# Sixteen bytes between two operands: moving the buffers of the 256-column matmuls within 256 bytes

## The reference

```python
xn = _layernorm(x, axis=-1)
x = x + attn(xn) + ffn(xn)

# attn: a linear-attention block, ending in an MLP
mlp = gelu(xn2 @ fc1_w + fc1_b, approximate=False) @ fc2_w + fc2_b     # 256 -> 1024 -> 256
# ffn: ternary weights (-1, 0, 1) with a scale for each output
h = silu(tlin(x, w1_w, w1_s)) * tlin(x, w2_w, w2_s)                    # 256 -> 1024
h = gelu(tlin(h, h1_w, h1_s), approximate=False)                       # 1024 -> 1024
h = gelu(tlin(h, h2_w, h2_s), approximate=False)                       # 1024 -> 1024
return tlin(h, w3_w, w3_s)                                             # 1024 -> 256
```

## The kernel before

| matmuls | held, streaming | lead |
|---|---|---|
| block products | `wb`, `xp` | 32 |
| down products | `a`, `wd` | 32 |
| MLP's second product | `h`, `wf2` | 32 |
| MLP's first product, 512 columns | `wf1`, `pm` | 0 |
| attention's output projection, 512 columns | `wo`, `pe` | 128 |
| attention's K projection, 256 columns | `pd`, `wq` | 0 |

## Time and profile before

### The profile page before, as it was taken

One profiled execution on the slowest core, in us unless ns is written; L12 is line 12 of the kernel. 1 busy time (PEld: TensorE's weight loads), 2 busy tenths in 40 slices (PEclk: granted clock), 3 DMA queues, 4 the chain that ended last, 5 costly groups with the idle time before them and its releaser, 6 DMA issues.

```text
span 1036.4 us, 17189 instructions
## 1 busy us (share of the span) xinstructions
PE 1002.4 (97%) x6628; PEld 899.7 (87%) x6628; DVE 747.5 (72%) x965; ACT 603.1 (58%) x875; POOL 239.5 (23%) x221
## 2 busy tenths in 40 slices
PE   3999999999999999999999999999999999999998
PEld 3778877888877788888899889989999999999998
DVE  6874688544537768988876586876878977877664
ACT  4788667667436375556555454555547654665444
POOL 3444245233504100000000131231301322112210
PEclk9999999999999999999999999999999999999999
DMA  8989715868686645534302773325593323222310
GB/s 308 419 249 369 230 51 204 302 195 234 222 331 215 211 139 187 184 102 166 119 22 82 269 259 102 107 77 183 183 384 125 122 82 123 94 83 83 108 42 22
DMA packets 68802, 181.20 MB, mean 175 GB/s; under 512 B 5056, under 2 KB 26176, under 8 KB 65088
## 3 DMA queue, kind: packets, MB, share of 16 engines
q1 hardware_dynamic: 68720, 180.08, 50.1%
HBM read 122.39 MB, written 66.06 MB: 182 GB/s over the span
## 4 chain that ended last, share of the span: by engine, by line
PE 68%; DVE 7%; issue 4%; ACT 3%; DMA 2%; POOL 0%; DVEq 0%; ACTq 0%
PE pr L2293 41%; PE pr L206 13%; PE pr L2489 9%; DMA h_s<-u 2%; DVE xp_lo L2021 1%; PE pr L2440 1%; PE pr L199 1%; PE pr L2271 1%; PE pr L192 1%; ACT u L1446 1%; DVE x L1572 1%; DVE u L2027 0%; PE pr L2433 0%; DVE tf L2005 0%; DVE tf L2009 0%
## 5 line engine op out<-in xcount | busy, mean ns | idle before, releaser
L2293 PE MATMUL pr<-xp_hi,wb 128*128 128x256 f32 x1344 | 315.5, 280 | 2.4 <-DVE u L2027 1.4
L2293 PE MATMUL pr<-xp_lo,wb 128*128 128x256 f32 x1344 | 314.9, 279 | 0.0
L2293 PEld LDWEIGHTS pr<-xp_hi,wb 128*128 128x128 f32 x1344 | 252.1, 188 | 4.5 <-issue 4.4
L2293 PEld LDWEIGHTS pr<-xp_lo,wb 128*128 128x128 f32 x1344 | 253.1, 188 | 0.0
L2293 PE MATMUL pr<-u_hi,ring 128*128 128x512 f32 x256 | 102.4, 400 | 1.8 <-POOL u_lo L950 1.0
L2293 PE MATMUL pr<-u_lo,ring 128*128 128x512 f32 x256 | 100.0, 391 | 0.0
L1430 ACT CAST xp_hi<-tf 128x1024 fp32r<-128x1024 f32 x48 | 50.3, 1047 | 56.9 <-PE pr L2293 21.4
L2021 DVE TENSOR_TENSOR xp_lo<-tf,xp_hi 128x1024 fp32r<-128x1024 f32 x48 | 61.9, 1289 | 19.5 <-ACT xp_hi L1430 19.4
L2489 PE MATMUL pr<-wf_hi,h_hi 128*128 128x256 f32 x256 | 74.6, 291 | 0.0
L2489 PE MATMUL pr<-wf_lo,h_hi 128*128 128x256 f32 x256 | 71.6, 280 | 0.0
L2489 PE MATMUL pr<-wf_hi,h_lo 128*128 128x256 f32 x256 | 71.4, 279 | 0.0
(11 more groups left out here) (236 smaller groups left out, 2507.2 us busy)
## 6 DMA issues: line engine op xcount, KB each, us to landing
ring<-w_s SPq DMA_DIRECT2D x42, 512.0 KB, 7.4
uf<-h_s SPq DMA_DIRECT2D x16, 1024.0 KB, 4.9
wb<-s_s SPq DMA_DIRECT2D x8, 1024.0 KB, 9.4
wb<-w_s SPq DMA_DIRECT2D x6, 1024.0 KB, 10.6
vw<-v_s SPq DMA_DIRECT2D x8, 514.0 KB, 6.9
xt<-x SPq DMA_DIRECT2D x8, 512.0 KB, 6.0
xn_s<-xh SPq DMA_DIRECT2D x8, 512.0 KB, 8.9
stage<-w_gated SPq DMA_DIRECT2D x2, 2048.0 KB, 13.5
```

Of the source, the lines that this page charges most:

```text
L2293: return e.matmul(bank, w.bitcast(dt), v_.bitcast(dt), start=first, stop=last, skip_group_check=True)
```

## The change

The lead of the block products, the down products and the MLP's second product becomes 16 instead of 32. Since placements are multiples of 32, a buffer that has to start at 16 modulo 32 is made four elements (16 bytes) longer, and its first four elements are skipped. Those buffers are `wb0` to `wb2`, `xp3` to `xp6`, `wd` and `wf2`. Addresses modulo 256, before and after:

| | held before | streaming before | held after | streaming after |
|---|---|---|---|---|
| products 0 to 2 | `wb` 128 | `xp` 160 | `wb` 144 | `xp` 160 |
| products 3 to 6 | `wb` 160 | `xp` 192 | `wb` 160 | `xp` 176 |
| down | `a` 128 | `wd` 160 | `a` 128 | `wd` 144 |
| MLP's second | `h` 160 | `wf2` 192 | `h` 160 | `wf2` 176 |

The high and low parts of `xp` and of `wf2` become two parts of one buffer, as far apart as before. Instructions, their order on each engine and their waits are the same; only addresses differ.

```diff
+PAST = 4
@@
-        wf2_hi, wf2_lo = (place(n, [P, KH, C], RD + 16448 + 8192 * i, F32R) for i, n in enumerate(("wf2_hi", "wf2_lo")))
+        wf2 = place("wf2", [P, PAST + 2 * KH * C], RD + 16416, F32R)[:, PAST:PAST + 2 * KH * C]
+        wf2_hi, wf2_lo = (wf2.rearrange("p (w k n) -> p w k n", w=2, k=KH)[:, i] for i in range(2))
@@
-        wb = [place(f"wb{p}", [P, HB, TOK], at_, F32R)
-              for p, at_ in enumerate((RA + 24832, RA + 33024, RA + 41216, RD + 32, RD + 8224, RD + 16416, RD + 24608))]
-        xp_at = (RG, RG + 8192, RG + 16384, RD + 49216, RD + 32832, RD + 57408, RD + 41024)
-        xp_hi = [place(f"xp{p}_hi", [P, HB, HT], at_, F32R) for p, at_ in enumerate(xp_at)]
-        xp_lo = [place(f"xp{p}_lo", [P, HB, HT], at_ + 4096, F32R) for p, at_ in enumerate(xp_at)]
+        wb_at = ((RA + 24832, PAST), (RA + 33280, PAST), (RA + 41728, PAST),
+                 (RD + 32, 0), (RD + 8224, 0), (RD + 16416, 0), (RD + 24608, 0))
+        wb = [place(f"wb{p}", [P, skipped + HB * TOK], at_, F32R)[:, skipped:skipped + HB * TOK]
+              .rearrange("p (m n) -> p m n", m=HB) for p, (at_, skipped) in enumerate(wb_at)]
+        xp_at = ((RG, 0), (RG + 8192, 0), (RG + 16384, 0),
+                 (RD + 49696, PAST), (RD + 32800, PAST), (RD + 58144, PAST), (RD + 41248, PAST))
+        xp = [place(f"xp{p}", [P, skipped + 2 * HB * HT], at_, F32R)[:, skipped:skipped + 2 * HB * HT]
+              .rearrange("p (w k n) -> p w k n", w=2, k=HB) for p, (at_, skipped) in enumerate(xp_at)]
+        xp_hi, xp_lo = [b[:, 0] for b in xp], [b[:, 1] for b in xp]
@@
-        wd_ = place("wd", [P, 2, PIECE], RG + 69632, F32R)
-        wd = wd_[:].rearrange("p a n -> p (a n)").rearrange("p (k n) -> p k n", k=KH)
+        wd_ = place("wd", [P, PAST + 2 * PIECE], RG + 69856, F32R)[:, PAST:PAST + 2 * PIECE]
+        wd = wd_.rearrange("p (k n) -> p k n", k=KH)
+        wd_ = wd_.rearrange("p (a n) -> p a n", a=2)
```

## The result

The changed kernel is slower: 1043.43 us in the median of six runs (1041.85 to 1045.65) against 1039.59 for the kernel before on the same chip (1038.81 to 1039.90), a ratio of 1.0040 with the interval 1.0029 to 1.0050. Forecast were 1030.5 us and a gain. In a later set of runs the ratio was 1.0038 (1.0025 to 1.0050).

What follows compares the result with a forecast made beforehand. TensorE's matmuls bound the kernel, busy 97% of the span. 3968 x (116.7 - 114.6) ns is 8.3 us off the profiled 1038.23, 1029.9, plus 0.6 for the median: 1030.5; likeliest range 1022 to 1035, 8 in 10 within 1014 to 1046.

Steps and rivals of the forecast that it cites:

- How many, and what of it counts: Block products 2688, MLP's second product 768, down products 512: 3968 matmuls on TensorE; one nanosecond each is 3.97 us.
- Does the lead matter at all?: Yes: the same matmul shape takes 120.0 ns at lead 0 in the K projection, 3.3 more than at lead 32.
- no change: Rival: the lead is not the cause, K projection's busier stage or strides are; 16 does as 32, 1038.9 us; chance 0.15.
- The bounds: Lead 16's matmul distance lies between 109.2 ns, read from the transposes, and 120.0 ns, read at lead 0.
- What I take between them: At lead 16 a matmul costs one full meeting and nothing for the second: 109.2 + 5.4 = 114.6 ns.
- meeting: Weight load and stream reach equal addresses modulo 256, twice per matmul; 5.4 ns each, 2.1 if cut by the load's end.
- the sum: Total over the three matmul kinds: 3968 x (116.7 - 114.6) = 8.3 us less.
- Alignment: Buffers 16 bytes past a multiple of 32 cost engines nothing, 0.3 us at most; DMA loads 0, upper end 2.1 us.
- the short lead: Rival: cost falls smoothly with lead, so 118.4 ns at lead 16, 6.5 us more, 1045.4; chance 0.22 for 1041 to 1052.
- The late load: Rival: a DMA load into a misaligned `wb` or `wd` ends late, up to 2.1 us slower; chance 0.01.
- Both meetings go: Rival: load and stream no longer disturb each other, floor reached, 29.8 us less, 1009; chance 0.12 for under 1022.
- What would show it: Trace signs: product starts 288 matmuls apart at 33.0 us instead of 33.61; step wrong if products 0 to 2 differ.

Runs made afterwards that it cites:

- lead 112: Changed kernel with all three matmul kinds at lead 112 instead of 16 and every held operand on a multiple of 32: 1030.61 us against 1039.29 before, ratio 0.9917.
- the probe: Only matmul streams, rest of the computation left out: 25 address pairs, four starts each, 96 matmuls per stream; 113.3 to 123.3 ns between starts, with one exception.
- the second probe: Only matmul streams again, rest of the computation left out: leads 16, 32, 112 and 192, 32 starts each; lead 112 settled at 113.3 ns in all 32.

## Why the prediction was wrong, step by step

- *How many, and what of it counts.* Right. 3968 matmuls without idle time, and the distance goes through to the end: at lead 112 the ledger gave 9.2 us less and the median fell by 8.7. VectorE did not become the bound.
- *Does the lead matter at all?* Right, and the K projection's 120.0 ns needs no busy stage: the probe has 120.0 at lead 0 in four of four starts, three of them with hardly any traffic. With that the rival "no change" falls too. The Trainium skill's "SBUF — State Buffer", Who interferes with whom, which stood behind this rival with its two independent read ports of a TensorE that waits on no one, does not agree with these streams: while a stream ran no other engine worked, and the distance went from 113.3 to 123.3 ns with the addresses.
- *The bounds.* Never was a settled distance under 113.3, so the 109.2 read from transposes was too low a floor for this shape (their row gives some 108); and 120.0 was no upper bound, since lead 4 gives 123.3.
- *What I take between them.* This step failed. It made of three leads a law, 5.4 ns for each meeting, and put lead 16 at 114.6 ns. There is no such law: by it leads 20 and 24 would lie between 114.6 and 116.7, and they gave 122.2 and 120.0; 112, whose second meeting comes 112 bytes before the end, would cost at least the 116.7 of lead 32, and is at the lowest distance of all, 113.3, in every start. A lead does not have a cost but a small set of distances, of which a stretch takes one and keeps it. For lead 16 with the held tile on a multiple of 32 these are 113.3, 116.7 and 118.7 in the probes, and this kernel got 116.7 and 118.7 nearly everywhere: 117.6 on average in products 3 to 6, where the sum has 114.6. The 116.7 that I read for lead 32 was one of two as well; the kernel before has 117.8 in some stretches.
- *Alignment.* For the engines and DMAs the zero was right: ScalarE's casts into `xp` take 1048 ns against 1047, VectorE's low parts 1289 and 1289, and the second loads of the moved `wb0` to `wb2` land 6.1, 6.6 and 8.0 us after their issue (6.1, 6.8 and 8.1 before). For TensorE it was wrong, and this is the second step that failed. I had read it from transposes, whose held `v` is misaligned at the lowest distance of the trace, but which stream 128 columns. For 256 columns a held tile 16 past a multiple of 32 costs 1.6 ns at lead 32 and 6.7 at lead 112. At lead 32 it loses 0.32% by itself; in the change, at lead 16, the medians with and without it put it at roughly half of the loss.
- *The rivals.* The sign was that of the short lead, and by luck its 118.4 ns at lead 16 is close to the 118.7 of one of the distances found. Its mechanism is refuted all the same: 48 is worse than 32 (118.3), 20 worse than 16, and 12 as good as 32. The late load did not happen. "Both meetings go" did not happen at lead 16 beyond single stretches at 113.3; the pair that settles there in every start is lead 112 with the held tile on a multiple of 32, and that it does so because nothing meets is not shown.
- *What would show it.* The prediction named products 0 to 2 unlike products 3 to 6 as a sign that its step is wrong, by a second operand off 32. That was there (118.7 and 117.6 ns on average), and should have had a price instead of a sentence: the misaligned tiles were part of the change.

Open are three things. Why just these distances, and why a multiple of 32, no run here tells. What chooses between the distances of a set when a stream begins is only partly known: what ran before has a say, but the same beginning gave three results. And whether the wider spread of the changed kernel's run times comes from that choice was not measured, since only profiled runs show distances.

## What to carry to other kernels

Where TensorE is the bound and every matmul brings its own held tile, the addresses of the two operands are a tuning parameter, worth 0.8% less to 1.6% more time in this kernel; read it from start-to-start distances, never from durations. Don't extrapolate it from two or three leads: run a probe over address pairs, several starts each, and choose a pair that settles at the same low distance in every start (here held on a multiple of 32, lead 112). A move that changes one lead can push the held tile off its multiple of 32 at the same time, so price the two apart.

## What the hardware showed that I had not expected

- In the probes, streams of matmuls with 128 x 128 held and 256 columns streaming settle, for a given pair of addresses, at one to three distances between 113.3 and 126.7 ns, at a granted clock of 1.00 throughout, and keep the one they have until the stretch ends: in 32 of 32 starts of lead 16 in the second probe the last quarter ran as the second did.
- The state crosses from one stretch to the next: products 3 to 6 ran at 116.8 or at 117.7 ns at identical addresses, depending on the products before them, and in the changed kernel two kinds of tile alternated to the end.
- Getting into the fastest state can take time: at lead 112 in the kernel the first ten or so matmuls of many runs take 114 to 124 ns each. In the second probe the first twelve steps average 117.2 to 117.5 ns with the beginnings b = 2 and 3, and 113.3 or 113.4 with b = 1.
